# An attention and gated feed-forward block: sums over values gathered by small DMAs, a sorted w1, a new order

## The reference

```
xn = layernorm(x)
q3, k3 = xn @ Wq.T, xn @ Wk.T            # (b, 8 heads, t, 3)
v = xn @ Wv.T                            # (b, 8 heads, t, 16)
scores = q3 . k3 * scale + (q3 . dir_h) * (k3 . dir_h)
attn = softmax(where(causal, scores, -inf))
attention = (attn @ v, heads side by side) @ Wo.T
h = bitlinear(xn, w_fc) + gate * (xn @ v_lora.T @ fast_b.T @ u.T)
ffn = bitlinear(relu(h) ** 2, w_proj)    # bitlinear: weights ternary times a row's scale
return x + attention + ffn
```

## Time and profile before

| | us |
|---|---|
| median of three runs | 151.14 |
| lowest and highest | 150.56, 151.51 |
| the profiled execution's time | 150.95 |
| span of the profile in it | 149.2 |
| PE, DVE, ACT, POOL busy | 144.6, 114.2, 113.1, 41.7 |

### The profile page before, as it was taken

The page is one execution under the profiler, slowest core; times in us unless marked ns, Lnnn a source line. Parts: engine busy times, 40 slices in busy tenths (PEclk is TensorE's granted clock), DMA queues, the critical chain, the costliest instruction groups (busy, mean ns, idle before and its releaser), DMA issues.

```text
span 149.2 us, 4312 instructions
## 1 busy us (share of the span) xinstructions
PE 144.6 (97%) x1812; PEld 84.5 (57%) x1812; DVE 114.2 (77%) x266; ACT 113.1 (76%) x243; POOL 41.7 (28%) x60
## 2 busy tenths in 40 slices
PE   7999999999999999999999999999999999999992
PEld 2463884643556555363544447854376247877992
DVE  1999996699999997999999999799826947401212
ACT  3159972677988998899998795499999999794110
POOL 4550184033000161508997010000000592300000
PEclk9999998699999999999999999999999999999999
DMA  4940001601000107161000010110101100101012
GB/s 123 303 117 2 4 0 29 113 4 35 0 4 4 35 0 145 28 112 35 7 2 4 0 35 4 35 42 0 35 4 35 23 17 4 35 4 37 2 35 70
DMA packets 15528, 5.70 MB, mean 38 GB/s; under 512 B 10349, under 2 KB 15381, under 8 KB 15509
## 3 DMA queue, kind: packets, MB, share of 16 engines
q1 hardware_dynamic: 15168, 5.26, 15.2%
q10 hardware_dynamic: 340, 0.17, 0.4%
HBM read 2.02 MB, written 1.05 MB: 21 GB/s over the span
## 4 chain that ended last, share of the span: by engine, by line
PE 84%; ACT 6%; DVE 4%; DMA 2%; POOL 1%; issue 1%; POOLq 0%
PE obank L1021 23%; PE bank L919 11%; PE bank L810 10%; PE bank L774 5%; PE bank L785 5%; PE bank L984 5%; PE bank L926 4%; PE bank L1031 3%; PE bank L1064 2%; PE bank L906 2%; PE bank L880 2%; DMA x_sb<-in_x 2%; PE bank L987 2%; ACT tern L642 2%; PE bank L1039 1%; PE bank L990 1%
## 5 line engine op out<-in xcount | busy, mean ns | idle before, releaser
L587 DVE TENSOR_REDUCE pm<-bank 128x1 f32<-128x512 f32 (+2 forms) x160 | 90.4, 629 | 7.3 <-PE bank L945 4.7
L704 ACT ACTIVATE Pr<-bank 128x512 f32<-128x512 f32 (+1 forms) x160 | 77.0, 569 | 8.7 <-PE bank L984 5.5
L1021 PE MATMUL obank<-Pr,V 128*17 128x128 f32 (+3 forms) x576 | 37.7, 382 | 0.0
L1021 PEld LDWEIGHTS obank<-Pr,V 128*17 128x17 f32 x576 | 12.9, 96 | 10.6 <-issue 7.2
L612 DVE TENSOR_TENSOR x_sb<-bank,x_sb 128x256 f32<-128x256 f32 x8 | 3.4, 425 | 19.9 <-PE bank L1064 19.7
L478 POOL CAST QT<-nmax 128x16 bf16<-128x16 f32 x8 | 2.0, 255 | 57.2 <-DVE nmax L592 57.2
L919 PE MATMUL bank<-xnT,w1T 128*128 128x512 f32 x32 | 17.6, 652 | 0.2 <-ACT w1T L659 0.2
L810 PE MATMUL bank<-w2T,r 128*128 128x128 f32 x128 | 16.2, 280 | 0.1
L810 PEld LDWEIGHTS bank<-w2T,r 128*128 128x128 f32 x128 | 14.9, 192 | 1.4 <-ACT Pr L704 0.9
L485 POOL TENSOR_TENSOR r<-r 128x1024 f32<-128x1024 f32 x8 | 15.0, 1898 | 0.0
L774 PE MATMUL bank<-k_sb 32*128 32x128 bf16 x256 | 14.5, 225 | 0.0
(11 more groups left out here) (114 smaller groups left out, 192.8 us busy)
## 6 DMA issues: line engine op xcount, KB each, us to landing
out_y<-x_sb SPq DMA_DIRECT2D x8, 128.0 KB, 1.8
x_sb<-in_x SPq DMA_DIRECT2D x3, 256.0 KB, 4.4
wfc_sb<-in_w_fc SPq DMA_DIRECT2D x1, 256.0 KB, 3.9
wpj_sb<-in_w_proj SPq DMA_DIRECT2D x1, 256.0 KB, 4.1
k_sb<-in_consts SPq DMA_DIRECT2D x1, 178.5 KB, 3.6
x_sb<-in_x ACTq DMA_DIRECT2D x1, 128.0 KB, 2.6
x_sb<-in_x SPq DMA_DIRECT2D x1, 128.0 KB, 2.4
vo_sb<-in_vo SPq DMA_DIRECT2D x1, 128.0 KB, 4.2
```

The source lines that it names most:

```text
L587: nc.vector.tensor_reduce(out=dst, in_=src, op=ALU.max, axis=AX.X).then_inc(v_free, 1)
L704: nc.scalar.activation(Pr[:, n % PSLOTS, j, 0:cols], src[:, 0:cols], ACT.Exp).then_inc(a_free, 1)
L1021: last = nc.tensor.matmul(obank[32 * h:32 * h + HD + 1, o:o + cols], values(at, HG * g + h), Pr[:, slot, h, first:first + cols], start=ste ...
```

## The change

For the three quarters that aren't last, PE's transposes oT and oB, DVE's small inversions and products and ACT's copy go. In their place the values of a head become 32 columns wide, 16 values and 16 columns of ones, so that a norm stands in 16 rows; after oc, item out issues eight DMAs on SP's queue, two for each head, that bring 16 rows of sums to `outs` and 16 rows of norms to `norm`, at the rows that the head has in the output matrix. When the quarter closes, item divide inverts `norm` (128x512) on DVE and multiplies on POOL; the y items read `outs`. oc waits for the gathers of pass c - 2. The last quarter keeps its transposes. The memset of the ones is one item in POOL's order instead of two ahead of it. Item w1 issues its four low-rank matmuls first, before the wait for the ternary weights, and then the four with the identity, in one accumulation group. `MERGE`, `BANKS` and `JOINS` are new, so all items stand in another order. In the core below the three strings are cut to their first lines.

```diff
-         "e": [("tail", q) for q in range(QUARTERS)],
+         "e": [("tail", 0), ("ones",)] + [("tail", q) for q in range(1, QUARTERS)],
@@
-        s["o"].append(("oT", c))
+        s["o"].append(("oT", c) if q == LAST else ("out", c))
         if c == closing(q):
-            s["o"] += [("oB", q), ("y", q, 0), ("y", q, 1)]
+            s["o"] += [("oB", q) if q == LAST else ("divide", q), ("y", q, 0), ("y", q, 1)]
@@
-MERGE = ("nnnzzzzzzzzzzzzzzwwnntnlttzzezltzztzzgglttikzzzxmliiimmmmmmzzzzmmmuammkemgguubmmmemiimpmmmdfkssssmmm"
...
+MERGE = ("zzzzzzzzzznnwnnnnwezztlttltttkgtzzzzllgzzzemmmmizzmmmugiigmuuexmmmmzzzzmmieaemmupmmzzbdmzmmmmmmiisss"
...
@@
-        V = sb("V", [P, NT, H * (HD + 1) + HD - 1])
-        heads = V[:, :, 0:H * (HD + 1)].rearrange("p n (h d) -> p n h d", h=H)
+        V = sb("V", [P, NT, H, 2 * HD])
@@
+        def gather(engine, c, h):
+            k, row = CLOSED.index(at_quarter(c)) % 2, (coords(c)[1] * HG + h) * HD
+            engine.dma_start(outs[row:row + HD, k, :], oT[32 * h:32 * h + HD, c % 2, :]).then_inc(gathered[c], 16)
+            engine.dma_start(norm[row:row + HD, k, :],
+                             oT[32 * h + HD:32 * h + 2 * HD, c % 2, :]).then_inc(gathered[c], 16)
@@ SP
+                elif kind == "out":
+                    c = item[1]
+                    k = CLOSED.index(at_quarter(c))
+                    sp.wait_ge(o_copied, c + 1)
+                    if k >= 2:
+                        sp.wait_ge(v_full, V_FULL[("y", CLOSED[k - 2], 1)])
+                    for h in range(HG):
+                        gather(engine, c, h)
@@ POOL
-            nc.gpsimd.memset(V[:, :, H * (HD + 1):], 0.0).then_inc(ones_ready, 1)
-            nc.gpsimd.memset(heads[:, :, :, HD:HD + 1], 1.0).then_inc(ones_ready, 1)
+                elif kind == "ones":
+                    nc.gpsimd.memset(V[:, :, :, HD:2 * HD], 1.0).then_inc(ones_ready, 1)
+                elif kind == "divide":
+                    pool.wait_ge(inverted, CLOSED.index(q) + 1)
+                    nc.gpsimd.tensor_tensor(outs[:, k, :], outs[:, k, :], norm[:, k, :], ALU.mult).then_inc(divided, 1)
@@ DVE
+                elif kind == "divide":
+                    for c in range(NC):
+                        if at_quarter(c) == q:
+                            dve.wait_ge(gathered[c], 16 * 2 * HG)
+                    nc.vector.reciprocal(norm[:, k, :], norm[:, k, :]).then_inc(inverted, 1)
@@ PE, w1
-                        pe.wait_ge(w1_ready, 1)
                         pe.wait_ge(a_free, A_FREE[("w", "lora_b")])
                         for j in range(HC):
-                            nc.tensor.matmul(o[:, j * P:(j + 1) * P], wfc_sb[:, j, :], ident[:, :], start=True, stop=False)
-                            last = nc.tensor.matmul(o[:, j * P:(j + 1) * P], v_sb, loraB[:, j * P:(j + 1) * P],
-                                                    start=False, stop=True)
+                            nc.tensor.matmul(o[:, j * P:(j + 1) * P], v_sb, loraB[:, j * P:(j + 1) * P],
+                                             start=j == 0, stop=False)
+                        pe.wait_ge(w1_ready, 1)
+                        for j in range(HC):
+                            last = nc.tensor.matmul(o[:, j * P:(j + 1) * P], wfc_sb[:, j, :], ident[:, :], start=False,
+                                                    stop=j == HC - 1)
@@ PE, pv
-                            last = nc.tensor.matmul(obank[32 * h:32 * h + HD + 1, o:o + cols], values(at, HG * g + h),
+                            last = nc.tensor.matmul(obank[32 * h:32 * h + 32, o:o + cols], values(at, HG * g + h),
```

More of the change, by code:

```diff
@@ L188, in takes_bank @@
 def takes_bank(x):
-    return x[0] in ("xT", "qk", "turn", "v", "w", "maxA", "maxB", "maxO", "maxD", "stD", "stO", "stA", "stB", "oT", "oB",
-                    "y0", "ffn") or x[0] == "y" and x[1] != LAST or x[0] == "mT" and x[1] in BY_PE
+    return x[0] in ("xT", "qk", "turn", "v", "w", "maxA", "maxB", "maxO", "maxD", "stD", "stO", "stA", "stB",
+                    "oT", "oB", "y0", "ffn") or x[0] == "y" and x[1] != LAST or x[0] == "mT" and x[1] in BY_PE
 def filled_for(x):
@@ L340, in build @@
         qm_ready = [sem(f"qm_ready{c}") for c in range(NC)]
-        pv_done, o_copied, squared, stored = (
-            sem(n) for n in ("pv_done", "o_copied", "squared", "stored"))
+        pv_done, o_copied, inverted, divided, squared, stored = (
+            sem(n) for n in ("pv_done", "o_copied", "inverted", "divided", "squared", "stored"))
+        gathered = [sem(f"gathered{c}") for c in range(NC)]
         def cols16(x):
@@ L593, in _ @@
                                             op=ALU.max, axis=AX.X, negate=True).then_inc(top_ready, 1)
+                elif kind == "divide":
+                    q = item[1]
+                    k = CLOSED.index(q) % 2
+                    for c in range(NC):
+                        if at_quarter(c) == q:
+                            dve.wait_ge(gathered[c], 16 * 2 * HG)
+                    nc.vector.reciprocal(norm[:, k, :], norm[:, k, :]).then_inc(inverted, 1)
                 elif kind == "oT":
                     c = item[1]
[L596 to L604 removed]
+                    g, o = coords(c)[1], filled(item)[:, :].rearrange("p (n h r) -> p n h r", n=TPC, h=HG)
+                    dve.wait_ge(divided, CLOSED.index(LAST) - 1)
+                    link(nc.vector.reciprocal(inv[:, g, :, :], o[:, :, :, HD]))
+                    nc.vector.tensor_tensor(on[:, :, g, :, :], o[:, :, :, 0:HD],
+                                            inv[:, g, :, :, None].to_broadcast([P, TPC, HG, HD]),
                                             ALU.mult).then_inc(v_free, 1)
@@ L787, in values @@
             def values(at, head):
[L789 removed]
+                return V[:, at, head, :]
             def rows_turned(c, half):
@@ L1060, in _ @@
                     pe.wait_ge(a_free, A_FREE[("w", "wvo")])
-                    pe.wait_ge(a_free, A_FREE[("oB", q)])
+                    if q == LAST:
+                        pe.wait_ge(a_free, A_FREE[("oB", q)])
+                    else:
+                        pe.wait_ge(divided, CLOSED.index(q) + 1)
                     for n in range(2):
                         at = (2 * h + n) * P
-                        last = nc.tensor.matmul(o[:, n * P:(n + 1) * P], onT[:, CLOSED.index(q) % 2, at:at + P],
+                        last = nc.tensor.matmul(o[:, n * P:(n + 1) * P], outs[:, CLOSED.index(q) % 2, at:at + P],
                                                 wvoT[:, 1, :], start=False, stop=n == 1)
```

48 lines of the change are left out of this document (20 added, 28 removed).

## The result

The changed kernel took 169.66 us (median of six runs, 167.61 to 170.62) against 150.95 for the kernel before on the same chip: the ratio is 1.120 with a 95% interval of 1.114 to 1.126. The forecast was 148.1 us, in 144.8 to 152.2. It was wrong in sign and by 21.6 us. Some kernels here have slower executions too, at another granted clock, so a ratio with an interval compares the fast ones alone, while a median is that of all executions.

The account below looks back on a forecast made before the run. PE and DVE were taken to hold each other until 108 us. From 150.95 us, less 6.0 (PE), plus 2.0 (DVE) and 1.0 (SP), came 147.95, or 148.1 beside the median; range 144.8 to 152.2.

Parts of the forecast that it names:

- PE relief of 6.0 us on the path: On PE, 36 transposes and lost time around them give 4.8 us, sorted w1 1.2; all subtracted from the span.
- DVE's reciprocal: Three 512-element reciprocals of 3.3 us each on DVE; divide.0 adds 2.0 us net before top.5.
- divide.1 and divide.3 "cost nothing unless late": These later divides fall where DVE has 10 us free out of 24, so they were counted at no cost.
- SP ahead of mT.5: Sixteen DMAs of out.2 and out.3 on SP delay mT.5 by 1.6 us; 1.0 us taken, bounds 0 and 1.6.
- The clock: Half-clock dip from 25 to 29 us costs 1.7 us; w1's change may remove or leave it; counted 0.
- two charges: The additions to the sum: 2.0 us for DVE before top.5 and 1.0 us for SP before mT.5.
- Start: V's memsets leave POOL's start, but cut.0 still waits for DVE's statistics; first maximum stays at about 12.7 us.
- w1's place: w1 now follows pass 1's maxima, ahead of stD.0; PE's wait for its inputs was put at 0 to 1.2 us.
- wide loads: PE's 576 weight loads, 17 to 32 columns, 13 ns more each, counted 0; rival with 7.5 us seen, chance 0.04.
- Nothing is left: Rival: bank hand-offs set the pace, DVE's net 5.9 us cancels PE's relief; 151.0 us, chance 0.21.
- Slower: Outcome of chance 0.17: PE waits at w1 (0.13, 152.8 us) or wider loads are seen (0.04, 155.6 us).
- My own sign of being wrong: Wrong if top.5 comes over 2 us later than before, PE stands at w1, or the reciprocal is short.

Follow-up runs that it names:

- e4: The kernel before with only w1 sorted (four low-rank matmuls first, then four with the identity): 149.42 us, ratio 0.990.
- e9: The kernel before with sorted w1, and 27 of 36 transposes left out (output wrong): 149.11 us, ratio 0.988.
- e13: The kernel before with sorted w1, and maxO's 64 reductions on DVE reading 384 of 512 columns: 148.81 us, ratio 0.984.
- e16: The kernel before with sorted w1, 27 transposes left out, maxO's reductions and 48 exponentials cut to 384 columns (output wrong): 148.70 us, ratio 0.980.
- e10: The kernel before with sorted w1, plus one unneeded 128x512 reciprocal on DVE right behind top.4: 153.84 us, ratio 1.020.
- e2: The changed kernel with out.2 and out.3 moved on SP ahead of the store of y.0.0: median 164.62 us, profiled execution 158.83.
- e3: The changed kernel with a copy in place of the reciprocals (values not divided) and out.2, out.3 ahead of the stores: 152.18 us, ratio 0.9993.
- e1: The changed kernel with a copy in place of the reciprocal in all three divide items (values not divided): 157.72 us, ratio 1.044.
- e7: The changed kernel with 18 filler matmuls on PE ahead of its wait for Qm of pass 5: median 170.42 us.
- e11: The kernel before with sorted w1 and values 32 columns wide, old transposes kept: median 157.58 us, two executions near 152.4, four near 157.7.

## Why the prediction was wrong

By its own steps:

- **PE relief of 6.0 us on the path: wrong, and the first step that failed.** The count of the work was right (36 transposes gone; w1 2.1 us). But only the w1 part was worth its time (1.1 us in e4), and 27 of the 36 transposes were worth 0.3 us of 3.0 (e9). I took 71.90 of 72 us busy as a full PE, after noting myself that it proves no such thing. I then named DVE as the other bound from its 95%; taking 8.5 us from it gave 0.6 us (e13), so that was no bound either. By these runs no engine's sum of work sets the pace; relief of all three at once brought 0.7 us by the median and at most 1.5 by the ratio (e16). What it is instead wasn't settled: hand-offs between engines in a fixed order are what is left over, argued and not shown.
- **DVE's reciprocal: size right, effect wrong.** 3.3 us was forecast, 3.35 measured; the smallest fixed part would have given 3.7. The row with 128 columns (0.94 us) and the one with 512 (3.35 us) give (3.35 - 0.94) / 384 = 6.3 ns an element, six times a reduction's 1.04. The Trainium skill's repeat count of 8 (VectorE: DVE Perf Modes, "First, the fixed hardware budget"), read as eight steps an element, had given an estimated 4.3 us; the trace doesn't agree with that reading. The step that failed is the next one: I added 2.0 us as net work before top.5, as though a block were the same as its length spread out. One block stops PE for 2 to 2.7 us, and costs 2.4 us against a copy with the clock held, 4.4 us in e10, and 6.6 us where the clock falls for 10 us. All three together cost 8.6 us with the clock held (e2 less e3, profiled executions) and 11.9 us in the changed kernel (e1), not 2.0.
- **divide.1 and divide.3 "cost nothing unless late": they were late.** DVE stood 3.85 and 12.41 us for their gathers, with reductions behind divide.1.
- **SP ahead of mT.5: mechanism right, size wrong.** The place, the sixteen DMAs and the absence of cover were named. I priced a gather at 0.45 us, from loads; one of 16 rows by 512 took 0.59, and 0.63 to the next. y.0.1's sum at 103.12 to the end of the queue at 114.5 is 11.4 us, not 7.6, and mT.5 went 4.85 us late, not 1.6. Moving these outs is worth 6.6 us (e1 to e3, the low clock behind the wait included), not 1.0.
- **The clock: a term put at 0, with bounds of 1.7 us either way.** I had the dip that before showed, but no rival in which the waits that the change makes bring new ones. Behind the first stall the low clock costs 4.2 us where it lasts 10 us (25.7 against 21.6), 2.6 in e7's execution and nothing in e2's; behind mT.5 it is within the 6.6 us above and can't be told from the wait. Even the price of the dip that I knew was too high: 0.6 us, not 1.7 (e4).
- **The sum again, with what was measured.** Without its two charges the prediction stood at 144.95. The profiled execution of e3 took 150.93, so none of the 6.0 us of relief came, not even the 1.1 that w1 brought by itself in e4; what takes that back isn't shown. Then come 8.6 for the reciprocals, 6.6 for mT.5, and the 3.6 left over for the clock of the first stall: 169.7, against 169.43 in the profiled execution. The last term is a remainder, so this closes by its making.
- **Start, w1's place, ACT, wide loads: about right.** w1 wasn't waited for; top.1 came at 29.38 against 32.02, so the start was ahead. The memset took 1.80 us, under the 5 that I allowed, but what I hadn't seen is that it holds up a DVE instruction by 1.1 us. A D step took 1.08 us against 1.07, and the wider loads a median of 110 ns against 97, the 13 ns more that were forecast.
- **The rivals.** "Nothing is left" (0.21) gave 151.0 and is what happens to PE's relief, as e3 shows, but not from DVE's work. "Slower" had 0.17, on w1 and the loads, neither of which occurred. The case that came about (a block on DVE or SP, PE idle, the clock down) was missing, although each of its parts stood in the text. My own sign of being wrong did show it: top.5 came 5.0 us later than before, where the limit was 2, and PE was busy 150.5 us, not 139.

## What to carry to other kernels

In a program whose engines each follow one fixed order, price a long instruction or a burst of DMAs by what stands behind it and by how many banks are still free, not by its length: 3.35 us in front of the banks that PE needed next cost 2.4 to 6.6 us, and sixteen small DMAs ahead of one transpose 6.6. Busy shares of 95 to 100% on two engines don't say that less work on either will help; leave some of that work out and time it before building what removes it. Where a change makes TensorE wait as it did here (1.99, 2.35, 2.72, 3.97 and 4.95 us, each with a lower clock in it or behind it in at least one profile), carry the lower clock as a case of its own, with a price and a chance: over 1.99 and 2.44 us it was also seen to hold.

## What was unexpected of the hardware

- After the same 1.99 us wait in the same place TensorE went on at a granted clock of 1.00 in e2's profiled execution, at a mean of 0.66 over 10 us in e7's, and at 0.50 for 10 us in the changed kernel's. Executions of e2 lie from 158.8 to 166.3 us, those of e11 near 152.4 and 157.7.
- While POOL set 128x2048 elements in 1.80 us, one short DVE instruction beside it took 1.23 to 1.48 us in place of 0.17 to 0.21 and ended with the memset (changed kernel, e2, e3, e11).
- A reciprocal on DVE took 0.25 us for 16 elements, 0.94 for 128 and 3.35 for 512, where a copy of 512 took 0.44.
- A DMA of 16 rows of 2 KB from SBUF to SBUF held SP for 0.59 us, more than a store of 128 rows of 1 KB (0.37 to 0.39 us), and landed in 2.0 us.
- Eight matmuls of 16 rows and eight of 128 took 2.1 us sorted and 3.3 us in alternation.
